# Mixer stage of a decoder block: VectorE's residual and its statistics placed ahead of the skip addition, the gating and the decay's logarithm

## What is computed

```python
zxBCdt = x @ in_proj_w.T                      # z | xc | B (8 heads) | C (64) | dt (64)
dt = softplus(Bm + dt_bias)
xc = silu(depthwise_causal_conv(xc, conv_w, conv_b))      # 4 taps, 512 channels
a_bar = exp(dt * -exp(A_log))
h = a_t * h + b_t * x_t;  y_t = einsum('bhdn,bn->bhd', h, c_t)     # scan over 256 rows
y = (y + xh * D_param).reshape(B_sz, L, D_INNER) * silu(z)
y = rms_norm(y, norm_w) @ out_proj_w.T
x = layernorm(x + y)
```

## Time and profile before

| | |
|---|---|
| median of 3 runs | 2794.33 us (2793.87 to 2794.64) |
| the profiled execution's own time | 2795.52 us |
| its span, first to last instruction | 2793.6 us |
| busy over the span | PE 85%, PEld 78%, DVE 69%, ACT 47%, POOL 47% |
| mean granted TensorE clock | 0.933 of full speed |

### The profile page before, as it was taken

The page is one execution under the profiler, slowest core; times in us unless marked ns, Lnnn a source line. Parts: engine busy times, 40 slices in busy tenths (PEclk is TensorE's granted clock), DMA queues, the critical chain, the costliest instruction groups (busy, mean ns, idle before and its releaser), DMA issues. The chain is left out here.

```text
span 2793.6 us, 60202 instructions
## 1 busy us (share of the span) xinstructions
PE 2362.6 (85%) x18124; PEld 2185.7 (78%) x18125; DVE 1927.8 (69%) x4967; ACT 1312.9 (47%) x2753; POOL 1318.2 (47%) x1450
## 2 busy tenths in 40 slices
PE   7999999999959999999999999999929999995000
PEld 6777777777738999999999999999928999995000
DVE  6888888888845666666666666666735777775444
ACT  4555555555524444444444444444405666663000
POOL 4666666666631222222222222222244777776776
PEclk9999999999969999999999999999969999997555
DMA  3011111111021111111111111111166778885454
GB/s 129 27 34 34 34 34 34 30 34 31 25 78 45 54 62 64 64 63 43 60 55 63 63 63 52 54 59 52 36 234 223 249 250 251 255 253 157 150 150 139
DMA packets 179190, 264.29 MB, mean 95 GB/s; under 512 B 34034, under 2 KB 139762, under 8 KB 179058
## 3 DMA queue, kind: packets, MB, share of 16 engines
q1 hardware_dynamic: 166002, 227.22, 25.3%
q0 software_dynamic: 13056, 35.67, 4.0%
HBM read 181.57 MB, written 81.26 MB: 94 GB/s over the span
## 5 line engine op out<-in xcount | busy, mean ns | idle before, releaser
L1273 ACT ACTIVATE b_qT<-b_ps_qk,b_bq_c 128x256 f32<-128x256 f32 x256 | 121.4, 474 | 360.8 <-PE b_ps_qk L1117 360.7
L1352 DVE TENSOR_REDUCE b_mx<-b_ps_s 128x4 f32<-128x308 f32 x256 | 122.0, 476 | 227.0 <-PE b_ps_s L1150 181.9
L1172 PE MATMUL b_ps_o<-b_vv,b_pT 77*128 77x65 f32 x2048 | 260.4, 270 | 0.0
L1172 PEld LDWEIGHTS b_ps_o<-b_vv,b_pT 77*128 77x128 f32 x2048 | 249.8, 192 | 4.6 <-issue 3.8
L568 DVE SCALAR_TENSOR_TENSOR a_conv<-a_xc_pad,a_cw,a_conv 128x256 f32<-128x256 f32 x384 | 224.5, 644 | 10.3 <-ACT a_conv L457 10.3
L1284 ACT ACTIVATE b_pe_<-b_sd 128x308 f32<-128x308 f32 x256 | 118.0, 461 | 225.9 <-DVE b_sd L1356 223.2
L1569 POOL TENSOR_TENSOR b_ve<-b_mv,b_ln_eps 128x1 f32<-128x1 f32 x64 | 12.2, 190 | 442.9 <-DVE b_mv L1395 442.9
L1150 PE MATMUL b_ps_s<-b_kz,b_qT 128*128 128x154 f32 x1024 | 188.9, 307 | 0.0
L1162 PE MATMUL b_ps_pT<-b_mk,b_pe_ 128*77 128x128 f32 x1024 | 155.5, 274 | 25.5 <-DVE b_pT L1362 17.2
L110 PE MATMUL b_ps_qk<-b_xT_hi,b_wq_hi 128*128 128x256 f32 x512 | 161.4, 315 | 18.3 <-DMA b_c_f<-in_ctxT 11.9
L110 PE MATMUL a_p<-a_xT_hi,a_w_hi 128*128 128x256 f32 x384 | 125.7, 327 | 51.4 <-DVE a_res L648 39.5
(11 more groups left out here) (255 smaller groups left out, 8464.8 us busy)
## 6 DMA issues: line engine op xcount, KB each, us to landing
c_w<-parts_scratch SPq DMA_DIRECT2D x79, 1024.0 KB, 5.0
c_xa<-sent_scratch SPq DMA_DIRECT2D x71, 256.0 KB, 3.1
made_scratch<-c_o_t SPq DMA_DIRECT2D x71, 256.0 KB, 4.9
parts_scratch<-b_w_cut SPq DMA_DIRECT2D x32, 512.0 KB, 4.9
a_xT_f<-in_xT SPq DMA_DIRECT2D x32, 256.0 KB, 3.1
a_x_f<-in_x SPq DMA_DIRECT2D x32, 256.0 KB, 2.7
x_scratch<-a_x_t SPq DMA_DIRECT2D x32, 256.0 KB, 2.2
b_xa<-x_scratch SPq DMA_DIRECT2D x32, 256.0 KB, 2.9
```

The lines of the kernel that those rows point to most:

```text
L1172: last = pe.matmul(ps_o[:, (HD + 1) * i:(HD + 1) * i + HD + 1], pT[:, u.par, i, :], vv[:, b.par, G * g + i, :], start=True, stop=True)
L1273: act.activation(qT[:, b.par, m, :], ps_qk[:, 0:L], ACT.Identity, bias=bq_c[:, m:m + 1])
L1352: dve.tensor_reduce(mx[:, u.par, :], s, AX.X, ALU.max).then_inc(s_mx, 1)
```

## The change

`residual` moves in VectorE's list from the last place to the place right behind `normalise`, ahead of `add_d`, `silu_conv` and `log_decay`. Its lag stays 2, so it works on the same sequence as before in every step. No instruction is added, taken away or changed, and the other four engines' queues stay as they are.

```diff
             run_steps(dve, n_seq, [
                 (prep_once, 0), (x_high_next, 0), (taps(0, 1), 0), (y_low, 2), (gate, 0), (bias_dt, 0), (mask_g, 1),
-                (taps(1, 2), 0), (weigh(0), 1), (weigh(1), 1), (taps(2, 3), 0), (normalise, 3), (add_d, 1),
-                (silu_conv, 0), (log_decay, 0), (residual, 2)], spare=2)
+                (taps(1, 2), 0), (weigh(0), 1), (weigh(1), 1), (taps(2, 3), 0), (normalise, 3), (residual, 2), (add_d, 1),
+                (silu_conv, 0), (log_decay, 0)], spare=2)
```

## The result

The changed kernel takes 2818.28 us (median of 4 runs, 2812.57 to 2821.39), against 2794.48 us for the kernel before (4 runs, 2793.87 to 2797.62): ratio 1.0081, 95% interval 1.0062 to 1.0100. The profiled execution took 2816.37 us with a span of 2814.6. The predicted 2811 lies 7 us short of it.

The account below looks back on a forecast made before the run. It took a GpSimd-VectorE loop from L754 to L754 to set the period: 24.55 against 24.02 us, 15.4 us over 29 steps plus 1 us at the ends, +16.4, giving 2811 us. Range 2792 to 2824, the forecast's own 2802 to 2817.

Parts of the forecast that it names:

- `in_bc` no longer waits for the residual: TensorE: residual complete at about 408.0 instead of 413.27, so in_bc never waits for it; 1.42 us idle before.
- `add_d` late by 1.9 us, `in_x` held back: VectorE's first L673 ends at 409.55 against 407.67; TensorE's in_x starts at 409.60 instead of 408.47.
- `join`: GpSimd: L748, L624, L752, L754 in turn take 1.53 + 1.08 + 1.14 + 1.37 = 5.12 us.
- the rival that would have been faster: GpSimd keeps its turn, L752 directly after L748: 23.44 us a step, 17 us less, 2777; chance 0.12.
- From L754 to the end of `y_low`: GpSimd and VectorE: L557, two L736, the taps between and after, then y_low; sum 6.30 us.
- From there on: After y_low: 0.05 us to decay(0), 3.08 to decay(1), 3.08 to weigh(1), 3.62 to normalise.
- the upper bound: weigh(1) to normalise may grow from 3.62 to 3.88 us beside L725, making the loop 24.72 us.
- The loop: One end of L754 to the next through GpSimd and VectorE: sum 24.46 us, taken 24.55, against 24.02 before.
- the lower bound: L748 may start 0.08 us behind its input instead of 0.26, making the loop 24.28 us.
- The order of turns: VectorE and GpSimd exclude each other, issue order deciding: L624 goes before L752; if GpSimd held on, 23.38 us.
- The end of the mixer: Step 2 pushes add_d up to 1.9 us without gain, last steps 0; 1 us taken for both ends.

Follow-up runs that it names:

- the sums behind `silu_conv`: Kernel before, with only the residual's two L648 moved between silu_conv and log_decay, statistics last; 2792.91 us, ratio 0.9982.
- with 16: Kernel before, with the whole residual moved between add_d and silu_conv; 16 of 29 steps long; 2812.15 us, ratio 1.0078.
- the cast moved: Kernel before, with normalise and both L648 ahead of taps(2, 3), statistics before log_decay, and x_high_next (L557) behind y_low; 2790.71 us, ratio 0.9984.
- The best kernel: Kernel before, with both L648 behind silu_conv, statistics last, and step_size moved between in_bc and turn_y on TensorE; 2776.8 us, ratio 0.9935.

## Why the prediction was right, and where it was short

- *`in_bc` no longer waits for the residual.* Right.
- *`add_d` late by 1.9 us, `in_x` held back.* Right. From L663's start to the end of the first L673 is 3.15 us (417.72 to 420.87; summed 3.21), 1.8 us more than the 1.33 before. TensorE waits 0.76 and 0.85 us ahead of `in_x` in the steps shown; I had 1.1.
- *`join`.* Right: 1.55, 1.08, 1.16 and 1.39 us (summed 1.53, 1.08, 1.14, 1.37). L624 went ahead of L752, which decides between the forecast and the rival that would have been faster.
- *From L754 to the end of `y_low`.* Right: 6.28 us (426.05 to 432.33) for a summed 6.30, piece by piece within 0.01. That both L736 are in the loop, the kernel with one of them shows.
- *From there on.* `decay(0)` follows `y_low` by 0.15 us (I had 0.05) and `decay(1)` follows it by 3.07 us (458.23 to 461.30, summed 3.08). `weigh(1)` comes 3.08 us behind that (464.38; summed 3.08) and `normalise` another 3.65 us (468.03; summed 3.62, with 3.88 as the upper bound).
- *The loop.* 24.51 us in the undisturbed steps, for a sum of 24.46 and a value taken of 24.55. The sum took L748's start 0.26 us behind its input in every step and the lower bound took 0.08; each is true of every second step, in the kernel before already.
- *The order of turns.* The rule of the Trainium skill ("SBUF — State Buffer", Who interferes with whom), that the order of issue decides which of the two engines blocks the other, holds in the changed kernel too: L624, which reads two tiles of SBUF, was issued at 421.98, while L748 ran, and was served before L752, issued at 422.38. The one case that the prediction called on, L557, has a single input, so that the rule as the prediction words it does not cover it; the order of issue held there too.
- *What is missing from the sum.* This is the term that was mis-sized. The prediction took TensorE's clock as full throughout, and so put at nothing what falls of it would cost. Eight stretches at half clock, 10.4 us by the step lengths, are the term it lacks. They stand between the predicted 16.4 us and the 24.66 us that the rows give; the loop term itself was 15.4 and is 14.2.
- *The end of the mixer.* I took 1 us for both ends together. From the residual in step 2 or 31 this can't be read off, as the residual stands elsewhere in the step; the mixer's last L663 ends at 809.3 before and 834.2 after, 24.9 us later, so the ends cost next to nothing.
- *The distance of 7 us.* It is in part luck. The mixer ends 24.9 us later where 16.4 were forecast, 8.5 more; what follows the mixer was 3.9 us shorter in the one profiled execution than in the other, which is within its spread and nothing that the change does.

What stays open is the cause of the half-clock stretches. Shown is that what TensorE does around `scores` and `decay(0)` bears on them. The cleanest pair is the order with the sums behind `silu_conv`, without and with `step_size` early: undisturbed steps of the same length, ten stretches and none in the profiled executions. Eleven dummy matmuls a step remove them too, and so does one L736 less; with 16 they are most frequent where the wait for `y_low` is longest. But the move of `step_size` took only one of eight away in the changed kernel, where the wait is 1.0 us, and one of four with the cast moved. The best kernel has waits of up to 0.7 us there and no stretch, and with five dummy matmuls they come with no idle time ahead. The wait is thus not the cause by itself, and the runs don't say what else is.

One rival is untested. In the changed kernel all steps do the same work to within 0.3 us, yet only some hold a stretch, and the eight begin 75.1 or 99.0 us apart, after three or four steps. Where a step lies in time thus seems to count, beside what it does. An edit that changes a step's length changes that as well, so of the experiments only those that keep the length (with and without `step_size` early) are free of it.

## What to carry to other kernels

When two engines serve each other in a ring, don't ask what the moved work releases, but what it now stands in front of, and follow the ring once round; here a wait of 1.4 us went away at one place, and an input came 1.8 us later at another. Where VectorE and GpSimd work side by side, look for instructions far longer than their peers that end just behind one of the other engine's: these are turns, and a late instruction takes its turns with it. Split a stage when only part of it releases someone: two of the residual's seven instructions, put where nothing waits behind them, together with `step_size` moved on TensorE gave 0.65%, and the whole stage cost 0.8%.

## What the runs showed of the hardware that I had not expected

- TensorE's granted clock can fall to half for a short stretch in a stage in which the engine is busy 93% of the time (596.52 of 640 us), with single waits below 1 us. In one such case it was busy for 2.90 of the 3.20 us ahead of the fall, in part with matmuls of 8 columns; in the kernel with five dummy matmuls it was busy for all 3.20. Each stretch made a step 1.3 us longer in the changed kernel.
- More work on the engine does not guard against it: the kernel with undisturbed steps of 23.3 us had ten, the kernel before with its 24.0 us none. With `step_size` in another place, the same 23.3 us had none in the profiled execution.
- A VectorE instruction that waits for its turn gets it between two GpSimd instructions issued back to back: the two L736 let L557 through before, and a tap at 428.09 to 428.37 after.
- An instruction of VectorE with one tile as input can wait for a turn too: `normalise` took 1.13 us instead of 0.40 beside L725 and ended 0.15 us behind it, and L557 took 1.41 us beside L736, where it takes 0.41 when nothing is in its way (in the kernel with L557 behind `y_low`). The residual's L648, with PSUM as one of two inputs, did not: its pair takes 0.86 to 0.88 us wherever it stands.
